# First graph layer of a two-model graph network: the segment sums with narrower rows, one-hots made by two engines, and weights copied by GpSimd

## The reference, cut to what matters

```python
q_dst = q[dst_e]
k_src = k[src_e]
logits = jnp.sum(q_dst * k_src, axis=-1) * scale + attn_bias
attn = _segment_softmax(logits, dst_e, E)      # per node: exp(l - max) / sum of exp
msg = v[src_e] * attn[..., None]
out = jax.ops.segment_sum(msg, dst_e, num_segments=E).reshape(E, EMBED)
return out @ Wo + bo
```

## Time and profile before

| | |
|---|---|
| three runs | 3136.4, 3146.5, 3149.1 us |
| median | 3146.5 us |
| the profiled execution, its own time | 3114.8 us |
| its span, first to last instruction | 3112.8 us |
| mean granted clock of TensorE | 0.65 of full speed |
| busy share of PE, DVE, ACT, POOL | 67%, 57%, 36%, 55% |
| stage B in the span | from 1492.0 to 1618.8 us |

### The profile page before, as it was taken

The page is one execution under the profiler, slowest core; times in us unless marked ns, Lnnn a source line. Parts: engine busy times, 40 slices in busy tenths (PEclk is TensorE's granted clock), DMA queues, the critical chain, the costliest instruction groups (busy, mean ns, idle before and its releaser), DMA issues.

```text
span 3112.8 us, 40117 instructions
## 1 busy us (share of the span) xinstructions
PE 2081.3 (67%) x10636; PEld 1720.0 (55%) x10636; DVE 1767.0 (57%) x6156; ACT 1134.2 (36%) x3023; POOL 1714.8 (55%) x1755
## 2 busy tenths in 40 slices
PE   6876767664355655551895777777786777777775
PEld 4544444443233333330783777677774677767775
DVE  9766656565467776558983444444446444343445
ACT  8433333331145445441123333333333333333331
POOL 1566666665666666660002666666662666666661
PEclk7555555555577777785897766666666666566665
DMA  2000000003222222230002333333333333333332
GB/s 76 4 5 4 5 4 4 4 5 102 70 60 66 65 64 67 65 54 3 1 1 98 111 109 112 109 109 113 111 107 81 111 109 110 110 108 112 109 105 32
DMA packets 114126, 209.58 MB, mean 67 GB/s; under 512 B 46139, under 2 KB 57213, under 8 KB 113533
## 3 DMA queue, kind: packets, MB, share of 16 engines
q0 software_dynamic: 69632, 146.42, 17.0%
q1 hardware_dynamic: 44284, 60.61, 6.3%
HBM read 193.30 MB, written 13.60 MB: 66 GB/s over the span
## 4 chain that ended last, share of the span: by engine, by line
another core or an unknown queue 20%; DVE 17%; PE 11%; issue 9%; ACT 3%; POOL 1%; DMA 1%; DVEq 0%; ACTq 0%; POOLq 0%
PE PS L1165 4%; DVE work L1319 4%; DVE red L1324 4%; DVE work L1336 3%; DVE work L1311 2%; PE PS L1393 2%; ACT kv L747 2%; PE PS L1403 2%; POOL arena L1299 1%; DMA arena<-kv_d,S 1%; DVE work L738 1%; PE PS L759 1%; PE PS L1405 1%; PE PS L1250 1%
## 5 line engine op out<-in xcount | busy, mean ns | idle before, releaser
L1299 POOL DMA_INDIRECT arena<-kv_d,S x528 | 512.4, 970 | 281.4 <-issue 151.2
L1403 PE MATMUL PS<-work,R 128*128 128x128 f32 x1760 | 560.5, 413 | 56.2 <-issue 49.3
L1299 POOL DMA_INDIRECT kv<-kv_d,S x352 | 343.0, 975 | 423.5 <-DMA kv_d<-arena 249.1
L924 POOL DMA_INDIRECT kv<-kv_d,S x440 | 425.1, 966 | 258.0 <-issue 132.7
L664 POOL DMA_INDIRECT sorted_d<-S,rows x416 | 419.4, 1008 | 265.9 <-issue 172.6
L1393 PE MATMUL PS<-arena,work 128*128 x1760 | 397.5, 397 | 241.6 <-DVE work L1319 206.5
L1393 PEld LDWEIGHTS PS<-arena,work 128*128 128x128 f32 x1760 | 343.6, 290 | 259.8 <-issue 259.8
L1360 ACT ACTIVATE R<-iota,gate 128x128 f32<-128x128 f32 x880 | 280.0, 388 | 445.8 <-remote 333.8
L1403 PEld LDWEIGHTS PS<-work,R 128*128 128x128 f32 x1760 | 406.2, 281 | 60.2 <-issue 59.5
L1405 PEld LDWEIGHTS PS<-wts,R 128*128 128x128 f32 x1760 | 401.1, 278 | 55.5 <-issue 55.5
L759 PE MATMUL PS<-kv,work 128*128 128x440 f16 x832 | 232.5, 440 | 243.8 <-DVE work L738 169.0
(11 more groups left out here) (269 smaller groups left out, 3173.8 us busy)
## 6 DMA issues: line engine op xcount, KB each, us to landing
work<-segT_d SPq DMA_DIRECT2D x165, 256.0 KB
kv<-kv_d,S POOLq DMA_INDIRECT x792
arena<-kv_d,S POOLq DMA_INDIRECT x528
sorted_d<-S,rows POOLq DMA_INDIRECT x416
kv_d<-arena SPq DMA_DIRECT2D x12, 512.0 KB, 2.9
sorted_d<-S SPq DMA_DIRECT2D x1, 2200.0 KB, 8.0
S<-sorted_d SPq DMA_DIRECT2D x1, 2040.0 KB
work<-in_edge_attr_dram SPq DMA_DIRECT2D x1, 1660.0 KB
```

The lines of the kernel that those rows point to most:

```text
L924: gp.indirect_dma_start(out=kv_near[:, g % SLOTS, j, :], out_offset=None, in_=kv0_d, in_offset=bass.IndirectOffsetOnAxis(ap=S0[:, t, 1:2]. ...
L1299: gp.indirect_dma_start(out=ring[s][:, j, :], out_offset=None, in_=kv1_d[l], in_offset=bass.IndirectOffsetOnAxis(ap=S1[:, t, 1:2], axis=0) ...
L1403: nc.tensor.matmul(PS[:, ds(blocks[g % 3][j] * DM, DM)], R[:, s, j, :], vw[:, n % 3, j, :], start=False, stop=True, skip_group_check=True)
```

## The change

A row of `vw0` has 72 columns and no zeros, so seven blocks fit in a bank and the 25 take four banks. The first three one-hots of a group come from one comparison by VectorE; the fourth is made by ScalarE in two steps, |node - iota| and then max(0, 1 - that), with two new semaphores, `s_dist0` and `s_Rl0`. The copy of the exponentials goes from ScalarE to GpSimd (`b_gpsimd`), behind its clearing of the two rows and ahead of its gathers for the second model. TensorE waits for four semaphores a group instead of three.

```diff
-VW0 = 96
+VW0 = D0 + H0
 PB = 512 // VW0
 NP = -(-NB // PB)
...
-        step0_all = take(NP - 1, T)
+        step0_all = take(4, T)
...
             for n in range(2):
-                nc.vector.memset(banks[n], 0.0)
+                done = nc.vector.memset(banks[n], 0.0)
+            done.then_inc(s_clear0, 1)
...
             dve.wait_ge(s_lines, 2)
-            nc.vector.memset(banks[4], 0.0).then_inc(s_clear0, 1)
...
         def b_vector(dve):
             dve.wait_ge(s_ex, 1)
-            vstep(nc.vector.memset(vw0[:, :, :, D0 + H0:VW0], 0.0))
+            most = TG - 1
             for g in range(NG):
                 since(dve, s_sum0, g - SLOTS + 1)
-                for j in range(TG):
-                    t = g * TG + j
-                    done = nc.vector.tensor_scalar(R[:, g % SLOTS, j, :], iota[:, :], seg0[:, t:t + 1], None,
-                                                   ALU.is_equal)
-                done.then_inc(s_R0, 1)
+                nc.vector.tensor_tensor(R[:, g % SLOTS, 0:most, :], iota[:, :].unsqueeze(1).to_broadcast([P, most, P]),
+                                        seg0[:, g * TG:g * TG + most].unsqueeze(2).to_broadcast([P, most, P]),
+                                        ALU.is_equal).then_inc(s_R0, 1)
                 since(dve, s_sum0, g - 1)
                 nc.vector.tensor_tensor(
...
         def b_scalar(act):
             for g in range(NG):
-                since(act, s_sum0, g - 1)
-                nc.scalar.copy(vw0[:, g % 2, :, D0:D0 + H0], S0[:, g * TG:(g + 1) * TG, 2:W0P]).then_inc(s_wb, 1)
+                t = (g + 1) * TG - 1
+                last = R[:, g % SLOTS, TG - 1, :]
+                since(act, s_sum0, g - SLOTS + 1)
+                nc.scalar.activation(last, iota[:, :], ACT.Abs, scale=-1.0, bias=seg0[:, t:t + 1]).then_inc(s_dist0, 1)
+                act.wait_ge(s_dist0, g + 1)
+                nc.scalar.activation(last, last, ACT.Relu, scale=-1.0, bias=ones[:, 0:1]).then_inc(s_Rl0, 1)
+
+        def b_gpsimd(gp):
+            gp.wait_ge(s_rows, 1)
+            gp.wait_ge(s_ex, 1)
+            for g in range(NG):
+                since(gp, s_wb, g)
+                since(gp, s_sum0, g - 1)
+                nc.gpsimd.tensor_copy(vw0[:, g % 2, :, D0:D0 + H0],
+                                      S0[:, g * TG:(g + 1) * TG, 2:W0P]).then_inc(s_wb, 1)
 
         def b_tensor(pe):
             pe.wait_ge(s_clear0, 1)
             for g in range(NG):
                 places = load_tensor(off0, g, NP * 512 - VW0)
                 pe.wait_ge(s_R0, g + 1)
+                pe.wait_ge(s_Rl0, g + 1)
                 pe.wait_ge(s_vw0, g + 1)
                 pe.wait_ge(s_wb, g + 1)
```

More of the change, by code:

```diff
@@ L51 @@
 FIRST = [OWN[C - 1]] + OWN[:C - 1]
-assert (2 + AHEAD) * EG * P // 2 <= (NP - 1) * T
+assert (2 + AHEAD) * EG * P // 2 <= 4 * T and NP <= 4
 assert NB % CB == 1 and N % P and ENDS[-1] == NEG and NPAD - N < P
@@ L336, in build @@
         s_R0 = sem("s_R0")
+        s_dist0 = sem("s_dist0")
+        s_Rl0 = sem("s_Rl0")
         s_vw0 = sem("s_vw0")
@@ L1567, in _ @@
             ones_gpsimd(gp)
+            b_gpsimd(gp)
             for l in range(LAYERS):
```

## The result

The changed kernel takes 3206.0 us in the median of four runs (3205.4 to 3210.0), the kernel before 3147.1 us. The ratio is 1.020, with a 95% interval of 1.018 to 1.023: **slower by 59 us**, where 3140.3 us, range 3126 to 3158, was forecast. The profiled execution took 3205.9 us with a span of 3203.0 us.

The account below looks back on a forecast made before the run. It took VectorE to set stage B's beat of 1.12 us a group, with TensorE's sequencer close behind. Saving 4.2 us on the beat and 2.0 once each, it forecast 3146.5 - 6.2 = 3140.3 us, range 3126 to 3158.

Parts of the forecast that it names:

- the 72 columns: Stage B, TensorE's array: 72 columns instead of 96 save at most 0.1 us a group, counted as nothing.
- 106 of the 110 groups go at this beat: Stage B: all but the first four groups keep the steady beat, 1.12 us before the change, 1.08 forecast after.
- VectorE's one-hots: Stage B: one comparison of 384 elements takes 0.56 us; VectorE then needs 0.81 us a group instead of 1.12.
- The fourth one-hot: Stage B, ScalarE: two activations take at most 0.83 us a group, covered by the beat; cost nothing.
- TensorE's sequencer at 1.05 to 1.09: Stage B: a second wait instruction adds 0.1 us; the sequencer's need, 1.05 to 1.09 us a group, is the largest.
- the beat alone: Stage B: a group takes 1.08 us, 0.04 less, over 106 groups: 4.2 us saved, with 3 and 7 as ends.
- The stages outside stage B: Rest of the kernel: a difference of more than 3 us there would show the prediction wrong altogether.
- The terms that belong to the four banks: Once each: sort's comparison and addition 1.0 us, clearing of bank 4 0.4, one bank less to read 0.2.
- GpSimd's copy: Stage B: the copy of 32 elements takes 0.26 us, with 0.24 and 0.94 as bounds, beside VectorE.
- Rival B: Stage B: GpSimd's copy becomes the bound, up to 1.44 us a group, 3178.5 us; a loss from 0.35; chance 0.13.
- Rival C: Stage B: VectorE and GpSimd take turns in full, 1.12 to 1.18 us a group likely, 3150.9 us at 1.18; chance 0.10.
- Rival A: Stage B: VectorE was the only bound, so the beat falls to 0.95 us, a gain of 20, 3126.5 us; chance 0.13.

Follow-up runs that it names:

- the kernel with the copy by itself: The changed kernel with rows of 96 columns, VectorE's product made to wait for GpSimd's copy: 3160.5 us in one execution, beside 3147.6 before.
- the profile with the 80 matmuls: The changed kernel with 96 columns, offsets of eight tiles per load and 80 matmuls of 256 columns added ahead of stage B: 3131.3 us, ratio 0.996.

## Why the prediction was wrong, step by step

**The step that failed** stands in the prediction under the 72 columns: "Half clock is no different: 1.71 / 8 = 0.213 is about twice 0.112." It asked what a narrow row costs at either clock, and not whether the clock would be the same. With it fell the assumption that "106 of the 110 groups go at this beat". None did: all behind the first two took 1.71 us, at half clock, 188 us in all. I had read in the earlier trace rows that the clock stood at half ahead of the stage and at 0.97 within, and in the earlier trace rows what half clock costs a group, 0.59 us, which is 106 x 0.59 = 62 us; the price of the miss stood in my own rows. No rival had the clock as its mechanism.

**VectorE's one-hots**: right. 0.563 for 384 elements (0.56 forecast), and VectorE idle for 0.2 us a group with 96 columns.

**The fourth one-hot**: right. Two activations of 0.40 each, and with 96 columns at full clock TensorE didn't wait for them behind the first group.

**72 columns worth nothing in array time**: right at half clock, where 72, 80, 88 columns take 1.707 us a group as 96 do. At full clock a group takes 1.10 us with either, and the weight loads within a group start 0.112 apart with either. (Stage B is 120.2 us with 72 columns and the clock up from the start, 122.4 with 96, where the first 6 us went at half clock.) Only the clock told them apart.

**TensorE's sequencer at 1.05 to 1.09**: right as the bound, at full clock, and the most useful part. With 96 columns the least time of a group is 1.06 and the median 1.08, as forecast for the beat; the mean over the stage is 1.10, so that the beat gave 0.02 a group and not 0.04. The sign that I had named for it, a first wait instruction that lasts little over 0.05, proves nothing: in the changed kernel it lasts 0.051 too. The forecast for the change, 3140.3 us, is met by the kernel with the width undone, 3139.5, but in part by luck. Its stage B is 122.4 us long instead of 124.8, 2.4 less, where 4.2 were forecast for the beat alone. The kernel as a whole gained 6.6 us, against 6.2 forecast, of which about 1.6 (the fifth bank, its clearing, the offsets' steps) belonged to the four banks; so some 4 us of the gain are not placed, and lie within the spread of the runs.

**The stages outside stage B** were to differ by no more than 3 us. That can't be read from single profiles, which lie 20 us apart there (3007 to 3027 us), and further with that of the kernel before (2988). The terms that belong to the four banks, 1.6 us, are too small to be seen, and no run shows them.

**GpSimd's copy**: mis-sized and harmless. 0.40 instead of 0.26, of which 0.215 is its own. Rival B's condition (from 0.35 on, always behind the product) isn't met: the copy ends 0.08 us behind the product that it waits for, since it stands in its queue while the product runs and not after it.

**Rival C**, taking turns, is true in part as a mechanism: the kernel with the copy by itself shows 0.18 us of waiting. The Trainium skill (SBUF — State Buffer, "SBUF: two separate sides") says that the later one blocks for the whole instruction of the earlier. The trace agrees that the later one waits, but not to the end of the other's record: then the copy would have taken 0.54 us, 0.325 of waiting and 0.215 of its own, and it took 0.40. It costs nothing in the beat, because the one that waits is GpSimd, which stands idle for 0.7 us a group, and VectorE's comparison is stretched by 0.01 only, where C's sign was 0.1.

**Rival A** fell: at full clock with 96 columns the beat is 1.10, not 0.95, and the sequencer has no slack. Even with the load paired and a third slot it stays at 1.02.

## What to carry to other kernels

Before narrowing the moving operand of a long stream of matmuls, look whether the stream begins at half clock and what raises it. Columns of zeros can be what brings TensorE to full clock: here 24 of them cost nothing in array time, and taking them away cost 59 us. And a busy share of 100% on TensorE doesn't say that it runs at full clock: read the granted clock beside it, stretch by stretch, and let "the clock stays as it was" be a step of the prediction with a rival of its own.

## What the runs showed of the hardware that I had not expected

TensorE ran 880 pairs of weight load and matmul back to back for 188 us at a granted clock of 0.50, the lower of its two levels (1.2 of 2.4 GHz), and it was never raised. The Trainium skill (TensorE: Matmul & The Clock Gate, "Part 1: The HAM clock gate") says that "the default state is throttled, and activity releases the throttle". Here matmuls without a gap were not enough: with the same weights and the same 1.71 us a group, 96 columns released it in each of six profiles, and 88 did not in the one that there is, nor, by their times, in its other executions. Why a wide row does it and a narrow one doesn't, no run here shows.

Raising and holding are two things. Rows of 72 columns held full clock for 120 us in one profile and lost it within 3 us of the start in another of the same program, and by their times the executions of that program fell into the two kinds almost evenly, 8 to 7. In the two profiles stage B is 120.2 and 186.1 us long. With 96 columns the clock fell at the start too, in the profile with the 80 matmuls, and came back after 3 us, and none of its executions was of the long kind. What makes the clock fall there in one execution and not in another is open.

A register load of eight offsets takes TensorE's sequencer 0.59 us, one of four 0.33.
